# Attention with routed experts on one core: another order of work at the entry of the attention stage, and 46 matmuls whose results nobody reads

## The reference

```
xn  = layernorm(x)                                  # over the 128 features
q, k, v = xn @ Wq, xn @ Wk, xn @ Wv                 # 16 heads of 8 features
q, k = q / |q|, k / |k|                             # per head
attn = softmax(causal(8 * q k^T))                   # 512 x 512 per head and batch
a   = (attn v) @ Wo
p   = softmax(xn @ Wr^T)                            # 8 experts
w   = the two largest of p, divided by their sum    # the others are 0
f   = sum over e of w_e * (gelu(xn @ W1_e^T + b1_e) @ W2_e^T + b2_e)
out = x + a + f
```

## Time and profile before

| what | value |
|---|---|
| median of 3 executions | 675.11 us (672.60 to 676.26) |
| profiled execution | 674.97 us |
| its span, first to last instruction | 673.2 us, mean granted TensorE clock 0.977 |
| PE busy | 615.6 us (91%), 7417 matmuls |
| DVE busy | 466.6 us (69%) |
| ACT busy | 449.7 us (67%) |
| POOL busy | 418.8 us (62%) |

### The profile page before, as it was taken

The page is one execution under the profiler, slowest core; times in us unless marked ns, Lnnn a source line. Parts: engine busy times, 40 slices in busy tenths (PEclk is TensorE's granted clock), DMA queues, the critical chain, the costliest instruction groups (busy, mean ns, idle before and its releaser), DMA issues.

```text
span 673.2 us, 21454 instructions
## 1 busy us (share of the span) xinstructions
PE 615.6 (91%) x7417; PEld 412.2 (61%) x7417; DVE 466.6 (69%) x1312; ACT 449.7 (67%) x689; POOL 418.8 (62%) x584
## 2 busy tenths in 40 slices
PE   2877558999999999999999999999999999999985
PEld 2755323444444447999999999999994444444432
DVE  7799987766667775454544446777665687897846
ACT  3999546888888885444444444444447888879892
POOL 6355637777777877775700016767755777777773
PEclk9899968999999999999999999999999999999997
DMA  5997684554455558945432235444534456564541
GB/s 158 293 286 229 194 257 107 96 118 105 100 131 125 126 112 174 243 130 144 129 82 71 71 80 120 115 113 118 121 98 81 95 124 119 136 134 98 121 107 48
DMA packets 186592, 89.36 MB, mean 133 GB/s; under 512 B 115456, under 2 KB 176032, under 8 KB 186400
## 3 DMA queue, kind: packets, MB, share of 16 engines
q1 hardware_dynamic: 178192, 70.70, 44.2%
q0 software_dynamic: 8336, 17.84, 9.8%
HBM read 30.17 MB, written 32.24 MB: 93 GB/s over the span
## 4 chain that ended last, share of the span: by engine, by line
PE 78%; DVE 5%; issue 4%; ACT 3%; POOL 1%; POOLq 0%; DVEq 0%; ACTq 0%
PE psum L1072 19%; PE psum L1060 18%; PE psum L952 17%; PE psum L920 8%; PE psum L880 7%; ACT prob L810 3%; PE psum L941 3%; PE psum L904 2%; PE psum L963 2%; PE psum L911 2%; POOL prob L664 1%; ACT prob L764 0%; DVE turn L1353 0%; PE psum L843 0%; DVE dup L1238 0%
## 5 line engine op out<-in xcount | busy, mean ns | idle before, releaser
L810 ACT ACTIVATE prob<-psum 128x1536 f32<-128x1536 f32 x192 | 267.0, 1454 | 56.7 <-PE psum L920 55.0
L820 ACT ACTIVATE prob<-psum,prob 128x256 f32<-128x256 f32 x284 | 117.5, 471 | 131.7 <-PE psum L1060 128.9
L648 POOL DMA_INDIRECT rows<-slot_y,idx x128 | 131.1, 1024 | 45.4 <-issue 26.4
L650 POOL DMA_INDIRECT slot_x<-rows,slots x128 | 128.1, 1001 | 35.8 <-issue 30.3
L952 PE MATMUL psum<-prob,v 128*18 128x448 f32 (+3 forms) x2048 | 137.5, 388 | 5.0 <-POOL prob L664 5.0
L1072 PEld LDWEIGHTS psum<-prob 128*128 128x128 f32 x1136 | 137.8, 192 | 3.6
L664 POOL TENSOR_SCALAR_AFFINE_SELECT prob<-prob 128x384 f32<-128x384 f32 (+2 forms) x224 | 104.8, 478 | 55.5 <-ACT prob L810 53.4
L1072 PE MATMUL psum<-prob 128*128 128x128 f32 x1136 | 138.1, 275 | 0.0
L1060 PE MATMUL psum<-xs,prob 128*128 128x256 f32 x568 | 134.6, 380 | 0.4 <-DVE xs L1466 0.4
L1060 PEld LDWEIGHTS psum<-xs,prob 128*128 128x128 f32 x568 | 102.5, 190 | 12.1 <-issue 0.6
L952 PEld LDWEIGHTS psum<-prob,v 128*18 128x18 f32 x2048 | 48.8, 98 | 92.7 <-issue 73.8
(11 more groups left out here) (159 smaller groups left out, 662.4 us busy)
## 6 DMA issues: line engine op xcount, KB each, us to landing
slot_y<-xs SPq DMA_DIRECT2D x71, 128.0 KB
xs<-in_L_attn_x SPq DMA_DIRECT2D x16, 256.0 KB, 3.9
prob<-in_L_ffn_W SPq DMA_DIRECT2D x16, 256.0 KB, 3.6
xn_rows<-prob SPq DMA_DIRECT2D x16, 256.0 KB, 2.7
xn_cols<-xts SPq DMA_DIRECT2D x16, 256.0 KB, 3.0
xt<-xn_cols SPq DMA_DIRECT2D x16, 256.0 KB
rows<-xn_rows SPq DMA_DIRECT2D x16, 256.0 KB
out<-acc SPq DMA_DIRECT2D x15, 256.0 KB
```

Source lines behind the costliest of these rows:

```text
L648: pool.indirect_dma_start(rows[:, j, c, t, :], None, done, where).then_inc(moved[j], 16)
L650: pool.indirect_dma_start(slot_x, where, halves_of_rows[:, j, 0, t, :], None).then_inc(moved[j], 16)
L810: act.activation(prob[:, KEPT[k], :], score[k % 2], ACT.Exp, scale=SCALE / UP ** 2)\
L820: act.activation(hs[:, s, c, :], psum[:, 2 * s + c // 2, (c % 2) * FT:(c % 2 + 1) * FT], ACT.Gelu, bias=ws[:, s, B1C + c:B1C + c + 1]).the ...
```

## The change

**PE at the entry.** A helper, `keep_going(bank, n)`, issues n matmuls of the identity with `barred` repeated to 512 columns, in f16; what they write is overwritten before it is read. 38 of them go between the transpose of b1 (L978) and the wait for `selected`, into bank 7. Eight more go behind the last chunk of values in batch 0, after a wait for the exps of units 0 to 10, into the first bank of the even units' scores.

**Waits.** Two semaphores are new. `counts_read` is raised by DVE after it has copied the counts (L1278), `ranks_read` after the second of the steps that read the ranks. `weigh(0, 0, 0)` waits for the first and `project(1, 0)` for the second, where both waited for `routed`. The clearing of `ps_o` (L1329) is gone.

**PE's order in batch 0** is written out (`first_batch`): projections behind scores 4, 6, 8, 10 (before: 3, 5, 7, 8) and value chunks 0 to 7 behind scores 3, 5, 6, 7, 9, 10, 10, 11 (before: 4, 5, 6, 7, 9, 10, 10, 11).

**DVE's order.** The copy of b1 goes ahead of the last `select`, `share_values(0, 0)` from behind the routing to ahead of the copy of `totals`. In batch 0 `evacuate(0, 0)` goes from behind `pick_tiles` to between `prepare(1, 1, 1)` and `prepare(1, 1, 2)`.

**POOL's order.** `pad_last_tiles()` goes from ahead of mask 0 to behind mask 1.

```diff
@@ gpsimd, body
-                if known(b, 0):
-                    pad_last_tiles()
                 for k in range(UN):
                     mask(b, k)
+                    if known(b, 0) and k == 1:
+                        pad_last_tiles()
                     if known(b, 0) and k == 5:
                         pool.wait_ge(routed, 1)
                         pool.wait_ge(padded, 16)
@@ tensor, project
                     if i == 0 and known(b, 1):
-                        pe.wait_ge(routed, 1)
+                        pe.wait_ge(ranks_read, 1)
@@ tensor, weigh
                     if known(b, 0):
-                        pe.wait_ge(routed, 1)
+                        pe.wait_ge(counts_read, 1)
@@ tensor, entry
+            def keep_going(bank, n):
+                pattern = barred[:].rearrange("p (a c) -> p a c", a=1).broadcast_to([P, 2 * TB, HP])
+                for _ in range(n):
+                    pe.matmul(bank, identh[:], pattern, start=True, stop=True)
+            keep_going(ps_pc, 38)
             pe.wait_ge(selected, T // ST)
...
             pe.wait_ge(proj_evac, TB)
+            scores(0, 0, 0)
+            scores(0, 0, 1)
+            def first_batch():
+                for k in range(2, UN):
+                    scores(0, 0, k)
+                    if k == 3:
+                        weigh(0, 0, 0)
+                    elif k == 4:
+                        project(1, 0)
+                    elif k == 5:
+                        weigh(0, 0, 1)
+                    elif k == 6:
+                        project(1, 1)
+                        weigh(0, 0, 2)
+                    elif k == 7:
+                        weigh(0, 0, 3)
+                    elif k == 8:
+                        project(1, 2)
+                    elif k == 9:
+                        weigh(0, 0, 4)
+                    elif k == 10:
+                        project(1, 3)
+                        weigh(0, 0, 5)
+                        weigh(0, 0, 6)
+                    elif k == 11:
+                        weigh(0, 0, 7)
+                        pe.wait_ge(exp_done, UN - 1)
+                        keep_going(score[0][:, 0:N], 8)
@@ vector, entry
-            for c in range(TOPK):
-                select(T // ST - 1, c)
             dve.wait_ge(btr_done, 1)
             dve.tensor_copy(wexp[:, :, B1C:W2C], psum[:, 5, 0:E * MC].rearrange("p (e c) -> p e c", e=E))\
                 .then_inc(bt_ready, 1)
+            for c in range(TOPK):
+                select(T // ST - 1, c)
+            share_values(0, 0)
             dve.wait_ge(counted, 1)
@@ vector, routing
             stepped(dve.tensor_copy(counts[:], ps_o[:, 0:2 * E].rearrange("p (c e) -> p c e", c=2)))
+            dve.sem_inc(counts_read, 1)
...
             stepped(dve.tensor_tensor(at_rank, ranks, of_halves(begins[:, 0:2]), ALU.add))
+            dve.sem_inc(ranks_read, 1)
...
-            dve.memset(ps_o, 0.0).then_inc(r_step, 1)
-            dve.wait_ge(r_step, next_step())
             dve.sem_inc(routed, 1)
@@ vector, body
-                if known(b, 0):
-                    share_values(0, 0)
...
                     prepare(b + 1, 1 - par, 1, second)
+                    if known(b, 0):
+                        evacuate(0, 0)
                     prepare(b + 1, 1 - par, 2, second)
...
                 if known(b, 0):
                     pick_tiles()
-                if known(b, 1):
-                    write_plan()
-                evacuate(b, 0)
+                else:
+                    if known(b, 1):
+                        write_plan()
+                    evacuate(b, 0)
                 divide(b, 0)
```

More of the change, by code:

```diff
@@ L253, in build @@
         r_step, counted, totals_read, placed = sems("r_step counted totals_read placed")
-        routed = sem("routed")
+        routed, counts_read, ranks_read = sems("routed counts_read ranks_read")
         residue_ready, later_ready = sems("residue_ready later_ready")
@@ L1007, in body @@
                 fresh = known(b, 0) or known(b, HALF)
+                if known(b, 0):
+                    first_batch()
+                    return
                 for k in range(UN):
                     scores(b, par, k)
-                    if k == 1 and not last and not known(b, 0):
+                    if k == 1 and not last:
                         project(b + 1, 0)
@@ L1017, in body @@
                         if not last:
-                            project(b + 1, 0 if known(b, 0) else 1)
+                            project(b + 1, 1)
                     elif k == 4:
@@ L1022, in body @@
                         if not last:
-                            project(b + 1, 1 if known(b, 0) else 2)
+                            project(b + 1, 2)
                         weigh(b, par, 1)
@@ L1028, in body @@
                         if not last:
-                            project(b + 1, 2 if known(b, 0) else 3)
+                            project(b + 1, 3)
                         weigh(b, par, 3)
-                    elif k == 8 and known(b, 0):
-                        project(b + 1, 3)
                     elif k == 8 and known(b, 1):
@@ L1041, in body @@
                             pe.wait_ge(plan_ready, 1)
-                        if not known(b, 0):
-                            out_project(b - 1, TB * (b + 1) if last else TB * (b + 2))
+                        out_project(b - 1, TB * (b + 1) if last else TB * (b + 2))
                     elif k == 10:
```

## The result

The changed kernel takes 678.04 us (median of 20 executions, 673.16 to 682.08) against 674.91 us for the kernel before (20 executions, 672.6 to 677.06): a ratio of 1.0044, 95% interval 1.003 to 1.0057. It is slower by 3.1 us, where 2.9 us less was forecast.

A forecast was written before the change was run, and what follows sets the result against it. The prediction took TensorE (PE), 78% of the chain, to bound the kernel. The entry's steps moved batch 1's first score matmul from 117.55 to 114.65, so 675.1 - 2.9 = 672.2 us, range 669.7 to 675.2.

The forecast's parts named there:

- The 38 matmuls: PE before the counting: 38 x 0.23 = 8.7 us at full clock, from 77.15 to 85.9, selection at 87.0.
- First exp: ACT in batch 0: first exp at 90.9 instead of 92.65 if the clock holds, 1.7 us earlier.
- the rival with 38 matmuls at half clock: PE before counting: the block takes 17.5 us, mark 4.7 us after the old one, 679.8 us; chance 0.05.
- Projections of batch 1: PE in batch 0: no wait for `routed`; the second waits some 2 us, for bank 7 until 100.35; `ps_o` transposed about 106.
- My rival on the clock: Clock low at the start of batch 0 after all: gain only 0.5 to 2.3 us; chance 0.20.
- The padding: POOL in batch 0: issued at 94.4, landing at 102.2 (101 to 103 allowed), first move about 102.3, later masks behind it.
- The end of batch 0: PE: chunk 7 waits for POOL masks, runs 111.8 to 112.8; eight matmuls take 1.85 us, to 114.65.
- the sum: Mark, the first score matmul of batch 1, moves from 117.55 to 114.65: 2.9 us gained, 672.2 us in all.
- the second rival: Padding lands by 100.5 or POOL's queue shrinks: gain 3.2 to 4.2 us, about 671.3 us; chance 0.28.
- Carried to the end: Behind the attention's entry: a train of PE work, so the mark's 2.9 us should all reach the end.
- one of my own signs of being wrong: Whole kernel: the forecast is wrong if the mark's shift isn't that of the end.
- the rival that nothing comes of it: Batch 1 gives the gain back through a POOL or DVE queue running over: 0 to 1 us gained; chance 0.05.

The follow-up runs named there:

- no38_at0: Changed kernel without the 38 matmuls, TensorE's code from batch 1 on at the same places as in `bef_at0`: 674.72 us.
- aft2_at0: Second run of the same code as `aft_at0`: 674.52 us.
- aft_c: Changed kernel, unchanged, one execution for a third trace: 682.28 us.
- aft_at0: Changed kernel with TensorE's code begun 92 instructions earlier in its block, so code from batch 1 on lies as in `bef_at0`: 674.69 us, 0.9994.
- bef_at0: Kernel before with TensorE's code begun at place 0 of a 256-instruction fetch block by one line at its head: 674.98 us, 1.0013.
- aft_at128: Changed kernel with TensorE's code from batch 1 on at the same places as in `bef_at128`: 680.01 us, 1.006 of the kernel before.
- bef_at128: Kernel before with TensorE's code begun at place 128 of a 256-instruction fetch block: 678.74 us, 1.0071.
- again: Changed kernel, unchanged, run again for a second trace: 676.94 us, 1.0014 of the kernel before.
- pad_first: Changed kernel with the padding put back ahead of mask 0 on POOL: 680.81 us, 1.0085 of the kernel before.
- no8: Changed kernel without the eight matmuls at the end of batch 0 and their wait: 683.45 us, 1.0107; with code placed as in `bef_at0`, 676.25 us.
- aft_d: Changed kernel, unchanged, one execution for a fourth trace: 680.09 us.
- no38: Changed kernel without the 38 matmuls ahead of the counting: 675.54 us, 0.9999 of the kernel before.
- masks_at0: `aft_at0` with the padding wait two units later and batch 0's moves behind more of the masks: 674.2 us, 0.9979 of the kernel before.

## Why the prediction was wrong

**The 38 matmuls: right.** 8.38 us for 8.7, at granted clock 1.00, counting at 87.21 for 87.0. **First exp: right**, 91.00 for 90.9, and the rival with 38 matmuls at half clock is out. That the block does what it should and still gains nothing shows in `no38_at0`. **Projections of batch 1: the times nearly right, the reason not.** The second one started at 100.88 for 100.35, the wait for `routed` is gone, and bank 7 is last, 0.41 us late. The 2 us of idle time that I expected before it were filled: PE ran at half clock from the 94th to the 101st us and reached that point with hardly any slack. `ps_o` was transposed from 107.01 us, for 106.05. My rival on the clock had it low from the first exp on; it fell later, but the rival's gain of 0.5 to 2.3 us at the mark is what the four traces show (0.72 on average).

**The padding: mechanism right, size off.** I took it to land at 102.2, between 8.2 us from issue and the end of the other queues' bytes. It took 8.5 us from its issue at 94.84, and GpSimd's first move came at 104.16 for 102.3. So it landed at 103.3, past the 101 to 103 that I had allowed. The time isn't fixed: 5.3 to 8.5 us in seven traces of the changed kernel, with or without the head line.

**The end of batch 0: missed.** Chunk 7 ran at 113.82 for 111.8, since its mask came late; at full clock, in `aft2_at0`, it waited longer and began at 113.54 all the same. From there to the mark it is 4.42 us, against 2.73 in `aft2_at0`: the half clock from the 111th to the 118th us stretched chunk 7 (1.91 for 1.06) and the eight matmuls (2.74 for 1.85), 1.7 us that the sum didn't have. (Chunk 6 was stretched as well, ahead of the wait for GpSimd, where it costs nothing.) Mark at 118.24 for 114.65, of which 0.42 us is a later L978. Two of the four traces have this second fall of the clock, the first and `aft_c`.

Where the clock held at the end of batch 0, in `aft_at0` and `aft2_at0`, the mark came 38.94 and 38.86 us after L978, against 37.74 forecast (114.65 - 76.91), 40.75 in the kernel before and 40.27 in `bef_at0`: a gain of 1.3 to 1.9 us of the 2.9. Two waits stand close together there. In `aft2_at0` the last is that for GpSimd; in `aft_at0` the padding landed after 5.8 us, chunk 7 ran at 111.60, and then PE waited for the transposes, of which the last was issued at 111.70 for 110.2 to 110.7 in the sum (PE's timeline of `aft_at0`):

```profile
111.60 1.06 PE L953 MATMUL psum<-prob,v 128*18 128x448 f32 x16 [0.36 <-POOL prob L664]
...
115.50 0.59 PE L905 MATMUL psum<-barred,identh 128*128 128x512 f16 x2 [1.01 <-issue]
```

So an earlier padding alone did not bring the 3.2 to 4.2 us of the second rival.

**Carried to the end: this step failed.** "Behind the entry of attention the kernel is a train of PE work, and what the entry gains or loses is carried to the end." It wasn't, twice over, and "if the mark's shift isn't that of the end" was one of my own signs of being wrong: over the traces the mark moved by -0.72 us, the median by +3.1. First, at equal places nothing is left at the end that stands clear of the noise (0.9994 for 1.0013, 1.006 for 1.0071): the rival that nothing comes of it, to which I had given 0.05 and 0 to 1 us. The traces, one of each kernel, differ on where it goes. `aft_at0` is 1.3 us ahead of `bef_at0` at the mark, 0.3 us at batch 2 and 0.45 us behind at batch 7 (157.13 us from L978 for 156.68), batch 1 alone giving back 1.0 us (20.60 for 19.62); `aft_at128` is 3.0 us ahead of `bef_at128` at the mark and still 3.3 us at batch 7 (156.62 for 159.89). Second, the row that the step rests on the earlier trace rows covers 200 to 300 us, not the rest: the train has points with hardly any slack, the transposing DMAs before each batch and each expert tile, and in the stages around them the changed kernel, without the head line, loses 1.76 + 1.53 + 1.82 us in its four traces. I costed the 92 added PE instructions as engine time only. They also move every later instruction in its fetch block, and a fetch can then fall among the transposes. At place 0, where it doesn't, the same change takes 674.5 to 674.7 us: 3.4 us of the median of 678.04 go with the place (2.3 us of the 676.94 of `again`, where the intervals overlap). That the place of the code changes the time is shown by the runs, by `bef_at128` above all; that a block's packet among the transposes is what delays them is read from traces and not shown by itself, with one exception on either kernel (batch 13 at 19.65 us in the first trace of after, at 19.71 us in `bef_at128`). `pad_first` shows that the place is not all.

The Trainium skill, "Runtime: NRT & Kernel Launch", section "Instruction fetch mechanics", says that code comes in blocks of 16 KiB over a queue of the engine's own and that crossing into the next block costs little, mostly hidden. The traces agree on the blocks (16384 bytes). On the cost the runs differ: moved blocks were worth 0.7% here (`bef_at128`), and in the traces the fetch's packet stands among transfers that the kernel waits for.

What stays open: why one batch from 2 to 4 takes 0.8 to 1.1 us more in most traces of changed kernels and in `bef_at128`; why `pad_first` is slower than `again`; why `aft_at0` spread over 670.12 to 679.62 us when the same code in `aft2_at0` stayed within 672.93 to 677.2 us; and whether one place of the code is better than all others, since only two were tried.

## What to carry to other kernels

When an edit adds or removes instructions ahead of long unrolled code, time it with the code behind it held at the same places of its fetch blocks, and at two places; otherwise the placement can be larger than the edit, as with `no8`, 1.0107 by itself and 1.0015 at equal places. A gain at the entry of a pipeline is worth what is left of it at the end: a mark where the edit ends doesn't tell, nor always one a few batches on (`aft_at128` was 3.3 us ahead at batch 7, and its executions are level with those of `bef_at128`). And before counting on a train of work, list its waits with under 1 us of slack, since each of them can turn a small disturbance into a pause with a low clock behind it.

## What the runs showed of the hardware that was not expected

Fetching TensorE's code is small in the page of the changed kernel (part 3: queue, packets, MB, share of the 16 engines):

```profile
q8 instruction: 37, 0.61, 0.4%
```

Yet one such packet of 16384 bytes takes about 1 us of a DMA engine, and where the code lies was worth 0.7% of the time in `bef_at128`. A pause of 2 to 3 us on PE can cost as much again behind it: in `no8` 3.02 us of waiting were followed by a granted clock of 0.54 over the next 4 us, in `aft_d` 2.70 us by 0.84 over a whole batch. Not every pause does: behind 2.17 us ahead of batch 14 in `again` and 2.14 us ahead of batch 1 in `no38` the granted clock was 1.00 over the batch, while 1.55 us in `masks_at0` were followed by 0.85.
